# A segment softmax whose running maxima pass between steps: scan carries read from PSUM, the last carry placed by a product with one, the rescale factor spread by a row of ones

## The chip, the cores and the metric

The kernel runs on one core of a Trainium2 chip. The metric is device time in microseconds (us) of the whole launch. Three runs of the kernel before gave 1501.42, 1502.57 and 1509.48 us; the median, 1502.57 us, is the time before.

## What is computed

A graph transformer layer and a mixture of eight small feed-forward experts, both with residuals, on 3125 nodes of width 256. The part that matters here is the attention over 53125 edges, sorted by destination:

```python
qi = q[dst]; kj = k[src]; vj = v[src]          # 4 heads of 64
alpha = jnp.sum(qi * kj, axis=-1) / 8.0
m = jax.ops.segment_max(alpha, dst, num_segments=n)
ex = jnp.exp(alpha - m[dst])
denom = jax.ops.segment_sum(ex, dst, num_segments=n)
out = jax.ops.segment_sum((ex / denom[dst])[..., None] * vj, dst, num_segments=n)
```

Then come the skip product, layer norms, a GELU feed-forward, the experts with batch norm and the last residual. The diff touches none of these.

## The kernel before

`build` runs three parts in sequence: `project` (keys and values to DRAM, order of the tiles), `attend` (attention, the only one that the diff touches) and `tail` (all the rest).

**Steps and groups.** `attend` walks 232 steps. A step covers two tiles of 128 edges and one block of 128 destination nodes. Eight steps make a group (`CP = 8`), 29 groups in all. In the code `j % CP` is the place of a step in its group, and `m` is the group before the current one. All loops are unrolled; each engine has its own order of instructions, written by hand, and semaphores join them. For each step:

- GpSimd (POOL) issues two indirect DMAs (line 690) that gather key and value rows into `ring`. It waits until VectorE has multiplied the step eight earlier (`s_prod`) and TensorE has summed the one 24 earlier (`s_agg`).
- TensorE (PE) expands the queries of the block to the edges, six products into `psQ` (line 784, function `expand`); in `rest` it then sums the weighted values of the step sixteen earlier into `psA` (line 810).
- VectorE (DVE) multiplies queries and keys (`prod`, line 982), makes the one-hot matrix `oh` for the sum (line 1000), adds `psA` to the accumulator (line 1016) and reduces `prod` to `alpha` (line 1022).
- ScalarE (ACT) weights the value rows (line 764).

**The chain of maxima.** While group `m+1` is multiplied, the segment maxima of group `m` are made in pieces, one or two a step, by `maximum` on VectorE and by `rest` on TensorE. TensorE transposes the scores to 64 rows (4 heads, 16 tiles) of 128 edges in `psM`; `F1` is a scan along each row; the last element of each row goes by a product into `tails`, a row in bank `psR`; a scan of `tails` gives `carry`; the product of `inh` (a copy of `carry`) with `one` turns it into a column of `psR`. VectorE copies that column to `cin` (line 927), and the scan `F2` starts each row from it (line 930). The same goes backward: `B1`, `heads`, `back`, `iv`, a column of `psR`, the copy `bin_` (line 954), the scan `Gm` (line 957). TensorE transposes `Gm` back (line 835), `dif` is the score less its maximum, and ScalarE takes its exponential. The first element of `tails` holds the last carry of the group before; VectorE writes it with a copy (line 953) behind the wait for `T_IV`.

**The rescale.** If the first segment of a group began in the one before, the accumulator's row is scaled by `fx`. VectorE makes a one-hot row `oh0` (line 950), a product of `oh0` with `fx` puts the factor on that node's partition (line 839), and `fac` adds `noh`, which is 0 at the node and 1 elsewhere (line 966).

**Order inside a step on VectorE.** After `prod` comes piece 0 of `maximum`, then `oh`, piece 1, the accumulator's addition, piece 2, and `alpha`. Pieces are named by (step in the group, piece): `cin` is at (3, 0); `oh0`, `tails` and `bin_` are at (5, 0); `F2` and `Gm` are at (3, 1) and (5, 1). On TensorE each piece follows the sums of its step, and the next `expand` follows the piece. `s_mv` counts VectorE's pieces, `s_mp` TensorE's.

Of the kernel before, what the change touches and what calls it, by code (L numbers as in the profile page):

```python
# [24 lines left out]
ALU = mybir.AluOpType  # L25
# [3 lines left out]
P = 128  # L29
N, HID, E = 3125, 256, 53125  # L30
H, D = 4, 64
FF = 4 * HID
NB, BP = 25, 128
# [12 lines left out]
W = LT * CP  # L46
CR = 4
RING = CR * CP
R = H * W
# [41 lines left out]
def project(nc, ctx, io, keep):  # L91
# [436 lines left out]
(V_ALPHA, V_F1, V_CARRY, V_INH, V_CIN, V_F2, V_B1, V_BACK, V_IV, V_FD, V_FMIN, V_OH0, V_NEXT, V_BIN, V_G,  # L528
 V_DIFF, V_FAC) = range(1, 18)
NV = 17  # L530
# [4 lines left out]
def attend(nc, ctx, io, keep):  # L535

    c = ExitStack()
    with c:
        def sb(name, shape, dt=F32):
            return c.enter_context(nc.sbuf_tensor(name, shape, dt))  # L540
# [11 lines left out]
        dstR, valN = keep["dstR"], keep["valN"]  # L552
# [8 lines left out]
        oh0 = sb("oh0", [1, BP])  # L561
# [9 lines left out]
        cin = sb("cin", [R, 1])  # L571
        bin_ = sb("bin_", [R, 1])
# [197 lines left out]
        def _(pe):  # L770
# [18 lines left out]
            def rest(i, j, fresh):  # L789
# [29 lines left out]
                if jj == 1:  # L819
                    pe.wait_ge(s_mv, NV * m + V_F1)  # L820
                    nc.tensor.matmul(tails[:, :, 1:W + 1], F1[:, P - 1:P], ident[0:R, 0:R], start=True, stop=True).then_inc(s_mp, 1)
# [14 lines left out]
                if jj == 6:  # L836
                    pe.wait_ge(s_fx, m + 1)
                    pe.wait_ge(s_mv, NV * m + V_DIFF)
                    nc.tensor.matmul(psM[0:BP, 400:400 + H], oh0[:, :], fx[:, :], start=True, stop=True).then_inc(s_mp, 1)
# [26 lines left out]
        def _(dve):  # L866
            nc.vector.memset(psM[0:R, 2 * P:2 * P + 1], 0.0).then_inc(s_set, 1)
            nc.vector.memset(tails, NEG).then_inc(s_set, 1)
            nc.vector.memset(heads, NEG).then_inc(s_set, 1)
            dve.wait_ge(s_set, 3)  # L870
# [24 lines left out]
            def maximum(i, j, part):  # L895
# [8 lines left out]
                def seen(n):  # L904
                    dve.wait_ge(s_mv, mv + n)
# [19 lines left out]
                if at == (3, 0):  # L925
                    dve.wait_ge(s_mp, mp + T_CARRY)
                    nc.vector.tensor_copy(cin[:, :], psR[0:R, 128:129]).then_inc(s_mv, 1)
                if at == (3, 1):
                    seen(V_CIN)
                    nc.vector.tensor_tensor_scan(out=F2[:, :], data0=nrow[:, 0:P], data1=psM[0:R, 0:P], initial=cin[:, 0:1],  # L930
                                                 op0=ALU.add, op1=ALU.max).then_inc(s_mv, 1)
# [15 lines left out]
                if at == (5, 0):  # L947
                    seen(V_FD)
                    nc.vector.tensor_scalar(fm[:, :], fd[:, :], 0.0, None, ALU.min).then_inc(s_mv, 1)
                    nc.vector.tensor_scalar(oh0[:, :], iotaF[0:1, 0:BP], dstR[0:1, bass.ds(W * m, 1)], None,  # L950
                                            ALU.is_equal).then_inc(s_mv, 1)
                    dve.wait_ge(s_mp, mp + T_IV)
                    nc.vector.tensor_copy(tails[:, :, 0], carry[:, :, W]).then_inc(s_mv, 1)
                    nc.vector.tensor_copy(bin_[:, :], psR[0:R, 384:385]).then_inc(s_mv, 1)
                if at == (5, 1):
                    seen(V_BIN)
                    nc.vector.tensor_tensor_scan(out=Gm[:, ::-1], data0=psM[0:R, P + 1:2 * P + 1][:, ::-1], data1=F2[:, ::-1],
                                                 initial=bin_[:, 0:1], op0=ALU.add, op1=ALU.max).then_inc(s_mv, 1)
# [4 lines left out]
                if at == (7, 0):  # L963
                    dve.wait_ge(s_mp, mp + T_FAC)
                    at_noh = (j // CP - 1) % CR
                    nc.vector.tensor_scalar(fac[:, :], psM[0:BP, 400:400 + H], noh[:, at_noh:at_noh + 1], None,
                                            ALU.add).then_inc(s_mv, 1)
# [1024 lines left out]
```

## Time and profile before

| | |
|---|---|
| median of three runs | 1502.57 us |
| profiled execution, its own time | 1504.69 us |
| its span, first to last instruction | 1502.9 us |
| TensorE busy | 1247.5 us, 83% |
| VectorE busy | 1078.1 us, 72% |
| GpSimd busy | 930.9 us, 62% |
| ScalarE busy | 810.3 us, 54% |
| TensorE's mean granted clock | 0.933 |

The profiled execution is 2.1 us above the median, and 1.8 us of it lie outside the span. Busy shares are means over the whole run. The attention runs from about 115 to 858 us of the span, so stretches of it are read apart. Where a row says that a wait was ended by "remote", the semaphore's update was recorded but could not be matched to an instruction; "issue" means that no recorded update ended it.

### The profile page before, as it was taken

What the parts mean: (1) busy time and instruction counts of PE and PEld (TensorE: products, weight loads), DVE (VectorE), ACT (ScalarE), POOL (GpSimd) and SP (SyncE); (2) the same over time, 40 slices, a digit from 0 to 9 for tenths busy, and PEclk for the clock granted to TensorE, in tenths of its full rate; (3) what the DMA queues carried; (4) which work ended last, traced back from release to release, by engine and by line L of the source; (5) the groups of instructions that cost most, each with busy time, mean ns of one, the idle gap of its engine ahead of it and who ended that gap; (6) DMA issues with size and microseconds to landing.
All of it is one profiled execution on the core that took longest, in us unless ns stands there. A gap on an engine that the chain in (4) does not pass through costs nothing. (4 is left out here: it accounts for less than half of the span.)

```text
span 1502.9 us, 24128 instructions
## 1 busy us (share of the span) xinstructions
PE 1247.5 (83%) x6835; PEld 966.9 (64%) x6835; DVE 1078.1 (72%) x2557; ACT 810.3 (54%) x2534; POOL 930.9 (62%) x883
## 2 busy tenths in 40 slices
PE   7988776677767677667657889999999999999998
PEld 3444454454445444444445578889898899999998
DVE  7647877777777787777868779886766665656655
ACT  1356766556666766566657654565543344444443
POOL 3365566656666665666665556866765477667765
PEclk9999879888898898998988999999999999999999
DMA  7477766666666666666665120101000000000002
GB/s 222 162 218 210 224 192 192 178 180 185 199 186 199 178 199 174 201 172 197 184 180 166 31 75 29 52 27 40 9 15 22 1 22 15 8 22 15 1 12 76
DMA packets 74072, 175.40 MB, mean 117 GB/s; under 512 B 11500, under 2 KB 36651, under 8 KB 73945
## 3 DMA queue, kind: packets, MB, share of 16 engines
q0 software_dynamic: 37632, 124.28, 29.6%
q1 hardware_dynamic: 34641, 48.25, 9.6%
q10 hardware_dynamic: 1672, 1.33, 0.3%
q8 instruction: 61, 1.00, 0.3%
q14 instruction: 66, 0.54, 0.1%
HBM read 159.91 MB, written 13.91 MB: 116 GB/s over the span
## 5 line engine op out<-in xcount | busy, mean ns | idle before, releaser
L690 POOL DMA_INDIRECT ring<-kv_rows,idx x464 | 466.5, 1005 | 296.4 <-issue 116.6
L764 ACT ACTIVATE ring<-ring 128x64 f32<-128x64 f32 x1800 | 442.1, 336 | 17.2 <-issue 16.1
L1287 POOL TENSOR_TENSOR wm<-k_gf,wm 128x512 fp32r<-128x512 f32 (+1 forms) x224 | 264.0, 1181 | 147.1 <-DVE wm L1786 147.1
L1386 ACT ACTIVATE k_gf<-psF,k_scT 128x512 f32<-128x512 f32 (+1 forms) x224 | 164.0, 733 | 258.3 <-PE psF L1557 258.3
L1786 DVE CAST wm<-k_gf 128x512 fp32r<-128x512 f32 (+1 forms) x224 | 168.8, 758 | 158.7 <-ACT k_gf L1386 157.0
L810 PE MATMUL psA<-ring,oh 128*128 128x260 f32 x912 | 274.1, 429 | 7.5 <-DVE k_acc L1016 7.1
L784 PE MATMUL psQ<-k_q,ohT 128*128 x1392 | 225.3, 304 | 58.7 <-issue 58.2
L982 DVE TENSOR_TENSOR prod<-psQ,ring 128x512 f32<-128x512 f32 x232 | 157.4, 678 | 89.5 <-remote 59.9
L784 PEld LDWEIGHTS psQ<-k_q,ohT 128*128 128x128 bf16 x1392 | 131.9, 105 | 115.7 <-issue 86.0
L810 PEld LDWEIGHTS psA<-ring,oh 128*128 128x128 f32 x912 | 178.0, 217 | 36.5 <-issue 8.5
L1022 DVE TENSOR_REDUCE alpha<-prod 128x8 f32<-128x512 f32 x232 | 155.6, 671 | 0.2
L1016 DVE TENSOR_TENSOR k_acc<-k_acc,psA 128x260 f32 x232 | 93.6, 403 | 15.4 <-PE psA L810 12.3
L1279 POOL TENSOR_TENSOR gT<-k_gf,gT 128x512 fp32r<-128x512 f32 (+1 forms) x56 | 74.1, 1325 | 38.8 <-ACT gT L1375 38.7
L1801 DVE SCALAR_TENSOR_TENSOR k_acc<-psO,wt,k_acc 128x256 f32<-128x256 f32 x200 | 84.8, 473 | 9.4 <-PE psO L1575 9.3
L1000 DVE TENSOR_TENSOR oh<-k_iotaF,k_dstR 128x256 f32<-128x256 f32 x217 | 88.3, 407 | 0.0
L1374 ACT ACTIVATE k_gf<-psF,b1c 128x512 f32<-128x512 f32 (+1 forms) x56 | 36.0, 642 | 77.3 <-PE psF L1512 77.2
L1532 PE MATMUL psO<-wm,gT 128*128 128x256 f32 x200 | 58.9, 294 | 0.0
L749 ACT ACTIVATE nrow<-psM 64x128 f32<-64x128 f32 x29 | 7.8, 270 | 93.4 <-remote 43.7
L1534 PE MATMUL psO<-wm,gT 128*128 128x256 f32 x200 | 57.0, 285 | 0.0
L1533 PE MATMUL psO<-wm,gT 128*128 128x256 f32 x200 | 56.9, 285 | 0.0
L846 PE MATMUL psA<-k_wqs,k_acc 128*128 128x512 f32 x100 | 49.3, 617 | 8.0 <-ACT qst L715 4.0
L755 ACT ACTIVATE ring<-dif 128x64 f32<-128x64 f32 x29 | 9.7, 334 | 85.6 <-DVE dif L961 60.8
(284 smaller groups left out, 2671.9 us busy)
## 6 DMA issues: line engine op xcount, KB each, us to landing
ohT<-step_destinations SPq DMA_DIRECT2D x29, 512.0 KB
ring<-kv_rows,idx POOLq DMA_INDIRECT x464
kv_rows<-kvst SPq DMA_DIRECT2D x25, 260.0 KB, 2.4
we<-in_L_ffn_W SPq DMA_DIRECT2D x16, 256.0 KB, 2.8
residual<-qst SPq DMA_DIRECT2D x25, 128.0 KB
xs<-in_x SPq DMA_DIRECT2D x2, 1024.0 KB, 8.8
resin<-residual SPq DMA_DIRECT2D x4, 512.0 KB
we<-in_L_ffn_Wo SPq DMA_DIRECT2D x8, 256.0 KB, 2.7
```

Of the source, the lines that this page charges most:

```text
L690: nc.gpsimd.indirect_dma_start(out=ring[:, LT * (j % CP) + k, j // CP:j // CP + 2, :].rearrange("p t e -> p (t e)"), out_offset=None, in_= ...
L764: last = nc.scalar.activation(row[:, 0:D], row[:, 0:D], ACT.Copy, scale=row[:, D:HW_])
L784: last = nc.tensor.matmul(psQ[j % NQ][:, k * HID:(k + 1) * HID], ohT[par][:, w * P:(w + 1) * P], q3[:, part, bass.ds(blk, 1), :].rearrange ...
L810: last = nc.tensor.matmul(psA[sj % NA][0:BP, 0:HALFW], onehot(b, k), ring[:, LT * (sj % CP) + k, sj // CP, :], start=(k == 0), stop=(k == ...
L982: nc.vector.tensor_tensor(prod[:, j % 2, :].rearrange("p (k d) -> p k d", k=LT), psQ[j % NQ][:, :].rearrange("p (k d) -> p k d", k=LT), ri ...
L1000: nc.vector.tensor_tensor(oh[:, sj % NO, :, :], iotaF[:, 0:BP].unsqueeze(1).broadcast_to([P, LT, BP]), dstR[:, bass.ds(LT * bo, LT)].unsqu ...
L1016: nc.vector.tensor_tensor(row, row, psA[sj % NA][0:BP, 0:HALFW], ALU.add).then_inc(s_acc, 1)
L1022: nc.vector.tensor_reduce(alpha[:, q % 2, :, LT * jj:LT * jj + LT].rearrange("p h w -> p w h"), prod[:, j % 2, :].rearrange("p (k h d) -> ...
L1287: nc.gpsimd.tensor_tensor(low[:, i % 2, m, 0:w], gf[:, n % 4, 0:w], high[:, i % 2, m, 0:w], ALU.subtract).then_inc(s_gl, 1)
L1386: nc.scalar.activation(gf[:, n % 4, 0:cols(g)], ps, ACT.Relu, bias=bias, scale=scale).then_inc(s_ev, 1)
L1786: nc.vector.tensor_copy((h1h if layer == 1 else h2h)[:, i % 2, m, 0:w], gf[:, n % 4, 0:w]).then_inc(s_dh, 1)
L1801: last = nc.vector.scalar_tensor_tensor(out=x1(t), in0=psO[n % 3][:, (u % 2) * HID:(u % 2 + 1) * HID], scalar=wt[:, t, e:e + 1], in1=x1(t) ...
```

## The change

Four VectorE instructions of each group go: the copies `cin` and `bin_` (the scans take their `initial` straight from the column in `psR`), the one-hot row `oh0` (a constant row of ones, set once, stands in its place, and `fac` takes the larger of the factor and `noh` in place of their sum), and the copy of the last carry into `tails`. In its place TensorE writes that element by a product of `carry` with `one`, just ahead of the product that fills the rest of `tails`, in 28 of the 29 groups. The waits for `T_CARRY` and `T_IV` move from the copies to the scans, one `oh` later. `fx` is at most 1, so the larger of `fx` and 0 or 1 is what the sum with the one-hot row gave.

```diff
@@ tensor engine, function rest
                 if jj == 1:
                     pe.wait_ge(s_mv, NV * m + V_F1)
+                    if m:
+                        nc.tensor.matmul(tails[:, :, 0], one[0:1, 0:1], carry[:, :, W], start=True, stop=True)
                     nc.tensor.matmul(tails[:, :, 1:W + 1], F1[:, P - 1:P], ident[0:R, 0:R], start=True, stop=True).then_inc(s_mp, 1)
...
-                    nc.tensor.matmul(psM[0:BP, 400:400 + H], oh0[:, :], fx[:, :], start=True, stop=True).then_inc(s_mp, 1)
+                    nc.tensor.matmul(psM[0:BP, 400:400 + H], orow[:, :], fx[:, :], start=True, stop=True).then_inc(s_mp, 1)
@@ vector engine, function maximum
-                if at == (3, 0):
+                if at == (3, 1):
                     dve.wait_ge(s_mp, mp + T_CARRY)
-                    nc.vector.tensor_copy(cin[:, :], psR[0:R, 128:129]).then_inc(s_mv, 1)
-                if at == (3, 1):
-                    seen(V_CIN)
-                    nc.vector.tensor_tensor_scan(out=F2[:, :], data0=nrow[:, 0:P], data1=psM[0:R, 0:P], initial=cin[:, 0:1],
+                    nc.vector.tensor_tensor_scan(out=F2[:, :], data0=nrow[:, 0:P], data1=psM[0:R, 0:P], initial=psR[0:R, 128:129],
...
-                    nc.vector.tensor_scalar(oh0[:, :], iotaF[0:1, 0:BP], dstR[0:1, bass.ds(W * m, 1)], None,
-                                            ALU.is_equal).then_inc(s_mv, 1)
+                if at == (5, 1):
                     dve.wait_ge(s_mp, mp + T_IV)
-                    nc.vector.tensor_copy(tails[:, :, 0], carry[:, :, W]).then_inc(s_mv, 1)
-                    nc.vector.tensor_copy(bin_[:, :], psR[0:R, 384:385]).then_inc(s_mv, 1)
-                if at == (5, 1):
-                    seen(V_BIN)
                     nc.vector.tensor_tensor_scan(out=Gm[:, ::-1], data0=psM[0:R, P + 1:2 * P + 1][:, ::-1], data1=F2[:, ::-1],
-                                                 initial=bin_[:, 0:1], op0=ALU.add, op1=ALU.max).then_inc(s_mv, 1)
+                                                 initial=psR[0:R, 384:385], op0=ALU.add, op1=ALU.max).then_inc(s_mv, 1)
...
-                                            ALU.add).then_inc(s_mv, 1)
+                                            ALU.max).then_inc(s_mv, 1)
```

VectorE's order before, in the sixth step of a group (here `oh` at line 950 is `oh0`, at line 1000 the one-hot matrix; `SCALAR_TENSOR_TENSOR` is how the order names a scan):

```order
L982 TENSOR_TENSOR prod<-psQ,ring 128x512 [waits s_alpha,s_qe,s_kv5]
L949 TENSOR_SCALAR fm<-fd 1x4 [waits s_maxv]
L950 TENSOR_SCALAR oh<-k_iotaF,k_dstR 1x128
L953 COPY psR<-carry 1x4 [waits s_maxp]
L954 COPY bin_<-psR 64x1
L1000 TENSOR_TENSOR oh<-k_iotaF,k_dstR 128x256 [waits s_agg]
L957 SCALAR_TENSOR_TENSOR Gm<-psM,bin_,F 64x128 [waits s_maxv]
L1016 ISA [waits s_acc,s_agg]
```

And now, in the changed kernel's own line numbers:

```order
L974 TENSOR_TENSOR prod<-psQ,ring 128x512 [waits s_alpha,s_qe,s_kv5]
L946 TENSOR_SCALAR fm<-fd 1x4 [waits s_maxv]
L992 TENSOR_TENSOR oh<-k_iotaF,k_dstR 128x256 [waits s_agg]
L949 SCALAR_TENSOR_TENSOR Gm<-psM,psR,F 64x128 [waits s_maxp]
L1008 ISA [waits s_acc,s_agg]
```

Three instructions are gone, and the wait for TensorE's piece (`s_maxp`) stands behind the one-hot matrix.

TensorE's order now, in the second step of a group, changed kernel:

```order
L807 MATMUL psA<-ring,oh 128x260 [waits s_acc,s_oh,s_pv]
L807 MATMUL psA<-ring,oh 128x260
L819 MATMUL psR<-carry,k_one 1x4 [waits s_maxv]
L820 MATMUL psR<-k_ident,F 1x4x16
L777 TENSOR_LOAD k_brow [waits s_prod]
```

The product with `carry` is new and takes over the wait for `F1`; the register load behind it belongs to the next step's `expand`.

## Rows read from the trace of the kernel before

**Rows 1.** Two stretches: busy us (count) of PE, PEld, DVE, ACT, POOL; clock, DMA share, GB/s.
```profile
115.00:858.00 743.00, 527.88 (x2703) 353.65 (x2701) 567.25 (x1517) 484.67 (x1986) 460.57 (x468) 0.88 0.63 181
860.00:1503.00 643.00, 623.29 (x3817) 566.31 (x3815) 437.84 (x820) 285.02 (x452) 423.40 (x353) 0.98 0.09 27
```
**Rows 2.** The same view, the middle of the attention.
```profile
200.00:800.00 600.00, 417.20 (x2177) 283.75 (x2175) 455.19 (x1214) 388.25 (x1616) 376.48 (x374) 0.88 0.65 187
```
**Rows 3.** Who VectorE waited for, 200 to 800 us: total, times, longest.
```profile
DVE prod L982 <- remote: 53.8, 22, 5.2
DVE prod L982 <- PE psQ L784: 15.4, 8, 2.4
DVE psR L953 <- remote: 14.7, 5, 4.1
DVE k_acc L1016 <- PE psA L810: 10.9, 9, 1.6
DVE cin L927 <- remote: 7.2, 3, 3.4
...
DVE F L914 <- ACT nrow L749: 4.8, 3, 3.3
...
DVE cin L927 <- PE psR L824: 2.7, 5, 1.2
```
**Rows 4.** GpSimd's gathers, 200 to 800 us: busy, mean ns, idle before them.
```profile
L690 POOL DMA_INDIRECT ring<-kv_rows,idx x374 | 376.6, 1007 | 223.8 <-issue 92.7 <-DVE prod L982 47.7 <-PE psA L810 37.4
```
**Rows 5.** VectorE in order of time, about 525 us: start, duration, idle before.
```profile
525.21 0.27 DVE L950 TENSOR_SCALAR oh<-k_iotaF,k_dstR 1x128 f32<-1x128 f32 x1
525.40 0.15 DVE L953 COPY psR<-carry 1x4 f32<-1x4 f32 x1
525.47 0.14 DVE L954 COPY bin_<-psR 64x1 f32<-64x1 f32 x1
525.54 0.40 DVE L1000 TENSOR_TENSOR oh<-k_iotaF,k_dstR 128x256 f32<-128x256 f32 x1
525.87 0.47 DVE L957 TENSOR_TENSOR_SCAN Gm<-psM,bin_,F 64x128 f32<-64x128 f32 x1
```
**Rows 6.** VectorE in order of time, about 443 us.
```profile
442.58 0.69 DVE L982 TENSOR_TENSOR prod<-psQ,ring 128x512 f32<-128x512 f32 x1 [3.17 <-remote]
443.19 0.14 DVE L927 COPY cin<-psR 64x1 f32<-64x1 f32 x1
443.26 0.41 DVE L1000 TENSOR_TENSOR oh<-k_iotaF,k_dstR 128x256 f32<-128x256 f32 x1
```
**Rows 7.** TensorE in order of time, 436 to 447 us.
```profile
435.94 0.85 PE L784 MATMUL psQ<-k_q,ohT 128*128 x6 [0.48 <-issue]
...
444.76 0.27 PE L828 MATMUL psR<-k_ident,B 64*1 64x64 f32 x2 [3.31 <-DVE B L934]
445.50 1.46 PE L784 MATMUL psQ<-k_q,ohT 128*128 x6 [0.47 <-issue]
```
**Rows 8.** Single lines of VectorE: ns min/median/max, first and last start us.
```profile
L950 DVE TENSOR_SCALAR oh<-k_iotaF,k_dstR x29: 267/268/353, 140.9 to 842.7; 1x128 f32<-1x128 f32 x29
L927 DVE COPY cin<-psR x29: 134/140/152, 131.3 to 839.8; 64x1 f32<-64x1 f32 x29
L930 DVE TENSOR_TENSOR_SCAN F<-nrow,cin,psM x29: 461/465/473, 131.4 to 840.2; 64x128 f32<-64x128 f32 x29
L914 DVE TENSOR_TENSOR_SCAN F<-nrow,psM x29: 401/402/413, 125.4 to 837.2; 64x128 f32<-64x128 f32 x29
```
**Rows 9.** VectorE by line and form, 200 to 800 us: busy, mean ns, idle before.
```profile
L953 DVE COPY psR<-carry 1x4 f32<-1x4 f32 x23 | 3.5, 150 | 17.0 <-remote 14.7 <-PE psR L831 1.3 <-issue 1.1
L927 DVE COPY cin<-psR 64x1 f32<-64x1 f32 x23 | 3.3, 143 | 12.4 <-remote 7.2 <-PE psR L824 2.7 <-issue 2.5
```
**Rows 10.** TensorE by line, 200 to 800 us: busy, mean ns, idle before.
```profile
L824 PE MATMUL psR<-k_one,inh 1*64 1x1 f32 x48 | 7.0, 213 | 6.8 <-DVE inh L924 6.3 <-issue 0.5
L821 PE MATMUL psR<-k_ident,F 64*1 64x64 f32 x48 | 7.0, 229 | 31.5 <-DVE F L914 28.4 <-issue 3.0
```

More of the change, by code:

```diff
@@ L525, in _ @@
                     backward(t - AT_ENDS - 1)
-(V_ALPHA, V_F1, V_CARRY, V_INH, V_CIN, V_F2, V_B1, V_BACK, V_IV, V_FD, V_FMIN, V_OH0, V_NEXT, V_BIN, V_G,
- V_DIFF, V_FAC) = range(1, 18)
-NV = 17
+(V_ALPHA, V_F1, V_CARRY, V_INH, V_F2, V_B1, V_BACK, V_IV, V_FD, V_FMIN, V_G, V_DIFF, V_FAC) = range(1, 14)
+NV = 13
 (T_IN, T_TAIL, T_CARRY, T_HEAD, T_IV, T_OUT, T_FAC) = range(1, 8)
@@ L560, in attend @@
         oh = sb("oh", [P, NO, LT, BP])
-        oh0 = sb("oh0", [1, BP])
+        orow = sb("orow", [1, BP])
         prod = sb("prod", [P, 2, LT * HID])
@@ L570, in attend @@
         Gm = sb("Gm", [R, P])
-        cin = sb("cin", [R, 1])
-        bin_ = sb("bin_", [R, 1])
         carry = sb("carry", [1, H, W + 1])
@@ L869, in _ @@
             nc.vector.memset(heads, NEG).then_inc(s_set, 1)
+            nc.vector.memset(orow[:, :], 1.0)
             dve.wait_ge(s_set, 3)
```

## The prediction

> **What bounds the kernel now.** The page's first part has no engine that fills the run, so I read its stretches next. After 860 us TensorE is busy 623 of 643 us; in the attention before it, 743 us, VectorE is the busiest with 567 us, and nobody is full [rows 1]. The change lies in the attention alone, so the 643 us behind it stay as they are, and the question is what sets the pace of the 743 us ahead of them.
>
> A group of eight steps takes 25.3 us: `cin` stands in the trace 29 times, first at 131.3 us and last at 839.8 us, and 708.5 / 28 = 25.3 [rows 8]. Between 200 and 800 us VectorE is busy 455.2 of 600 us [rows 2], so 19.2 us of each group, and idle 6.1 us. Its idle time comes in few, long pieces: 30 waits of up to 5.2 us ahead of `prod`, 9 of up to 1.6 us ahead of the accumulator's addition, some in the chain of maxima [rows 3]. One of them can be followed. VectorE starts `prod` at 442.58 us after 3.17 us of nothing [rows 6]; the queries it needs stand on TensorE from 435.94 us on, for 0.85 us [rows 7]. TensorE itself then sits 3.31 us, until VectorE has made `B1` for it [rows 7]. So TensorE's result became visible late, by a cause that these rows do not name, and then each engine stood and waited for the other. Outside such pieces VectorE works without a gap.
>
> GpSimd's gathers are not what is late. Of its 223.8 us of idle time, 92.7 us are the spacing of its own issue, and most of the rest it waits for `prod` or for the sums to free a place in the ring [rows 4]. It follows the others. I read the attention as paced by VectorE's work plus the late pieces.
>
> **The change, part by part.** *Removed from VectorE.* In the sixth step `oh0` starts at 525.21 and the one-hot matrix at 525.54: the three small instructions take 0.33 us of VectorE's queue [rows 5]. In the fourth step `cin` starts at 443.19 and the next one at 443.26: 0.07 us [rows 6]. That makes 0.40 us a group, and 29 x 0.40 = 11.6 us. Their own durations are longer, 0.27 + 0.15 + 0.14 us [rows 5] and 0.14 [rows 6], because neighbours overlap; 29 x 0.70 = 20.3 us is the upper bound, if nothing overlapped. The lower bound is 0: all of it disappears into the idle time. VectorE is free of idle for 455.2 / 600 = 0.76 of the stretch [rows 2]. I take that share as what passes to the end: 0.76 x 11.6 = 8.8 us.
>
> *The two waits move behind `oh`.* VectorE was idle 17.0 us ahead of `tails` and 12.4 us ahead of `cin` in 23 groups [rows 9]. The one-hot matrix holds the queue 0.33 us, from 525.54 to 525.87 [rows 5], and can now be made during such a wait. Thirteen waits at the two places have a row: 5 and 3 that were long, and 5 of up to 1.2 us [rows 3]; together 24.6 of the 29.4 us. Hidden are 13 x 0.33 = 4.3 us, times 29 / 23 groups 5.4 us. If the other 4.8 us of waiting were hidden whole as well, it would be 9.1 x 29 / 23 = 11.5 us, the upper bound; the lower is 0. I take 0.76 of the 5.4 us, as above: 4.1 us. No engine waits longer for the moved things: `F2` and `Gm` came behind `oh` before too, and `oh` itself comes sooner for TensorE's sum.
>
> *The scans with a start value in PSUM.* No row shows one. `F1`, with a constant, takes 402 ns; `F2`, with a start value in SBUF, 465 ns [rows 8]. If a PSUM value were as cheap as a constant, two scans a group would give 29 x 2 x 0.063 = 3.7 us more. If it cost a whole read of the same column, as `cin` does in 140 ns [rows 8], they would take back 29 x 2 x 0.14 = 8.1 us. I take 0, since the nearest row is the same scan with another start value, and it already reads its data from PSUM. The Trainium skill, page "VectorE: DVE Perf Modes", section "The TRN2 errata — SBUF-src ops pay a fixed extra latency per instruction", speaks against the change here: it gives a VectorE instruction 58 cycles fixed from SBUF and 120 from PSUM at 0.96 GHz. If a start value in PSUM were charged like that, an estimate from the page is 62 / 0.96 = 65 ns a scan, 3.7 us in all to take back, and the median would come out at 1494 us. No run here shows it yet.
>
> *The new product on TensorE.* Its kin are the one-element products: 213 ns a pass [rows 10], and the two passes of the product at 444.76 take 0.27 us together [rows 7]. 28 x 0.27 = 7.6 us is the upper bound. It stands at a place where TensorE waits for VectorE, 31.5 us ahead of the products with `F1` in this stretch [rows 10], and behind it the next `expand` starts only after 0.47 us that the sequencer spends on its register [rows 7]. `carry` has been ready since the group before. It delays `tails` by up to 0.27 us, and the scan of `tails` comes a whole step later on VectorE. I take 1.0 us for all groups; the bounds are 0 and 7.6. If the cover goes, because TensorE is the late one in that step, it costs the 0.27 us.
>
> *At no cost:* `max` for `add` in `fac` is the same instruction, and the product with ones reads 128 values as `oh0` did. The one `memset` is outside the loop. ScalarE and GpSimd have the same order as before.
>
> The sum: 8.8 + 4.1 + 0 - 1.0 = 11.9 us. From the profiled execution's own 1504.69 us that gives 1492.8. It lies 2.1 us above the median of the runs, so the median should be 1490.7, which I call 1491 us. About 0.5%, 7.5 us, is what a measurement of this kernel tells from no change: faster means under 1495, slower over 1510.
>
> **The rivals.**
>
> *A, the sum holds (0.46): 1487 to 1495, likeliest 1491.* For it: VectorE is gapless between the late pieces.
>
> *B, nothing that can be measured (0.32): 1496 to 1504.* The late pieces, 6.1 us of each group, might end by something that does not depend on VectorE's work. Then a VectorE that is done 0.4 us sooner waits 0.4 us longer. ScalarE's `nrow` holds up `F1` in 3 waits, 4.8 us [rows 3], and the DMA queues are busy 0.65 of the stretch [rows 2]: such causes would swallow the gain. Only the matrices made under a wait would be left, 0 to 4 us, and the PSUM start value could eat that too. Time 1500. Against it: 39 waits have their row ahead of `prod` and the addition, for 24 groups of eight steps [rows 3], so most steps have none, and in those VectorE's work counts in full.
>
> *C, slower (0.10): 1511 to 1530.* A wait takes the place of the removed work. A faster VectorE frees the ring sooner, the gathers follow closer on each other, and DMA's share, 0.65, rises. If the late results of TensorE go with busy DMA queues, there will be more of them. One costs about 3.2 us, as ahead of `prod` at 442.58 [rows 6]. Four more in 29 groups eat up the 11.9 us; from six more on the kernel is slower by over 0.5%, and ten more, one in three groups, give 1491 + 32 = 1523. For it: the late result at 442.58 has no other cause in these rows. Against it: VectorE's speed changes by under 2%, and gathers would come that much closer only.
>
> *D, faster than the sum (0.12): 1478 to 1486.* The engines stand and wait for each other, and TensorE's clock pays for it: 0.88 in the attention against 0.98 behind it [rows 1]. At half speed the six products take 1.46 us and not 0.85 [rows 7], 0.6 us more. A share of 0.24 at half speed makes 0.88. If shorter waits took it to 0.20, that is 0.04 x 232 = 9 steps less at half speed; with the sums, which are longer than the queries, some 1.5 us each, 14 us of TensorE, of which I would see half: 1491 - 7 = 1484. The Trainium skill's page "TensorE: Matmul & The Clock Gate", section "HAM oscillation — how this bites in real kernels", has the rule that a TensorE that idles falls to half its clock. By that rule the rows agree: the six products at 445.50 come behind an idle 3.31 us and take 1.46 us.
>
> **How the numbers follow.** Likeliest is A, so 1491. The range takes in A and B, most of D and none of C: 1482 to 1505, with some 0.15 to 0.2 outside. Faster: A's 0.46 (of which a little is above 1495) and D's 0.12, 0.57. Slower: C's 0.10. Within 0.5%: 0.33.
>
> **What would show it.** In the changed kernel's profile: VectorE's busy time down by some 10 us in the attention; the spacing of `fm` to `oh` in the sixth step 0.07 us; the scans `F2` and `Gm` at 465 ns, or over 500 if PSUM is dear. The group's period should be 24.9 us. If it is 25.3 with VectorE's idle time up by the same 0.4, it was B. If VectorE's long waits are more in number, it was C. The clock at 0.90 or more would be D. I am wrong in the sum if the start value in PSUM costs more than 0.2 us a scan, or if the long waits go by the clock on the wall and not by steps.

## The result, and the profile after

The changed kernel took 1531.13 us (median of 4 runs, 1526.77 to 1535.13), the kernel before 1501.99 us beside it (4 runs, 1498.76 to 1509.48): a ratio of 1.0199, interval 1.0167 to 1.0231. It is 29 us slower, where 1491 us was predicted. The profiled execution has a time of 1534.81 us and a span of 1533.0 us, 30.1 us more than before.

The chips differ, and this has to be said ahead of everything else. On some the kernel before takes 1501 to 1503 us, as above (the same in two later series on one chip); on three others it takes 1359 to 1361 us. I call the first **late chips** and the others **prompt chips**, for a reason that the traces show further down. A ratio is always to the kernel before on the same chip and in the same series; it can differ by up to 0.3% from the quotient of the two medians.

The same stretches of the changed kernel as in [rows 1, 2]: busy us (count) of PE, PEld, DVE, ACT, POOL; then clock, DMA share, GB/s. The last stretch is TensorE's 643 us behind the attention.

```profile
115.00:858.00 743.00, 526.97 (x2636) 359.07 (x2637) 531.19 (x1333) 459.22 (x1892) 443.67 (x436) 0.82 0.63 181
200.00:800.00 600.00, 418.39 (x2134) 290.31 (x2131) 426.55 (x1074) 366.98 (x1539) 362.65 (x358) 0.82 0.62 180
890.00:1533.00 643.00, 621.30 (x3817) 564.60 (x3816) 440.40 (x820) 285.50 (x453) 426.95 (x353) 0.99 0.09 27
```

What follows the attention is as it was: TensorE is busy 621 of the last 643 us, before 623 of 643 [rows 1]. The loss is in the attention, and there less got done in the same time: GpSimd issued 358 gathers in 600 us and not 374 [rows 4].

The two scans that now start from PSUM, by line (nanoseconds least/median/most, first and last start in us):

```profile
L927 DVE TENSOR_TENSOR_SCAN F<-nrow,psR,psM x29: 465/467/477, 132.5 to 870.7; 64x128 f32<-64x128 f32 x29
L949 DVE TENSOR_TENSOR_SCAN Gm<-psM,psR,F x29: 468/469/479, 142.2 to 873.9; 64x128 f32<-64x128 f32 x29
```

They take 467 and 469 ns; with a start value in SBUF it was 465 [rows 8]. The first and last start give the group's period: (870.7 - 132.5) / 28 = 26.4 us, where it was 25.3 and 24.9 was forecast.

What GpSimd waited for stands in one row of each kernel, the gathers' over the whole run (busy, mean ns | idle ahead of them, and what ended it). First the kernel before:

```profile
L690 POOL DMA_INDIRECT ring<-kv_rows,idx x464 | 466.5, 1005 | 296.4 <-issue 116.6 <-DVE prod L982 59.4 <-ACT idx L727 50.6
```

And the changed kernel:

```profile
L687 POOL DMA_INDIRECT ring<-kv_rows,idx x464 | 471.4, 1016 | 319.9 <-issue 120.2 <-ACT idx L724 104.5 <-DVE prod L974 40.2
```

GpSimd is busy 4.9 us longer and idle 23.5 us longer ahead of its gathers, together 28.4 of the 30.1 us. This sum shows no cause: GpSimd issues from one end of the attention to the other, and whatever holds it up, its busy and idle time add up to that length. The releasers say more. Its waits for VectorE's `prod` became shorter, 59.4 to 40.2 us, and those for TensorE's sums too, 39.8 to 11.0 us; the unmatched ones ("remote") grew from 15.7 to 29.8 us. What grew by far the most is the wait for `idx`, from 50.6 to 104.5 us. `idx` is the table of row numbers of a group of eight steps that ScalarE makes (line 724), one group ahead. The number of such waits stands in the same view by that line, "who waited for it". Before:

```profile
L727 ACT ACTIVATE idx<-k_srcI x29: 199/203/217, 69.9 to 795.4; 128x16 int32<-128x16 int32 x29
...
  POOL ring L690: 50.6, 16
```

And in the changed kernel:

```profile
L724 ACT ACTIVATE idx<-k_srcI x29: 198/202/216, 70.0 to 825.8; 128x16 int32<-128x16 int32 x29
...
  POOL ring L687: 104.5, 26
```

GpSimd ran out of indices in 16 of 29 groups before, and in 26 of 29 now.

Who waited for whom in the changed kernel, 200 to 800 us (total, times, longest):

```profile
ACT nrow L746 <- remote: 118.4, 22, 6.3
DVE prod L974 <- remote: 101.8, 31, 5.3
...
POOL ring L687 <- ACT idx L724: 82.2, 21, 4.1
...
DVE F L914 <- ACT nrow L746: 19.8, 10, 3.1
DVE Gm L949 <- remote: 19.8, 8, 4.2
```

In [rows 3] `prod` had 22 such waits, 53.8 us. The same view of the kernel before has two more rows, which neither the rows ahead of the prediction nor its argument took up:

```profile
ACT nrow L749 <- remote: 43.7, 9, 6.3
...
POOL ring L690 <- ACT idx L727: 32.6, 12, 4.1
```

`nrow` on ScalarE now waits 118.4 us for TensorE's transposes under this name, and 2.5 us in a wait that names them; before it was 43.7 us so, 31.4 us in waits that name them and 11.3 us under "issue". One of these waits shows the whole thing. ScalarE (start, duration, what it did, in brackets the idle time ahead and what ended it):

```profile
443.13 0.24 ACT L728 ACTIVATE stc<-k_startN 128x64 f32<-128x64 f32 x1
449.59 0.27 ACT L746 ACTIVATE nrow<-psM 64x128 f32<-64x128 f32 x1 [6.22 <-remote]
449.77 2.00 ACT L761 ACTIVATE ring<-ring 128x64 f32<-128x64 f32 x8
451.68 0.20 ACT L724 ACTIVATE idx<-k_srcI 128x16 int32<-128x16 int32 x1
```

TensorE, the transposes that it waits for, and the products with the queries that the late `prod` multiplies:

```profile
444.68 0.27 PE L813 MATMUL psM<-k_ident,alm 128*64 128x128 f32 x1
444.79 0.27 PE L814 MATMUL psM<-k_ident,stc 128*64 128x128 f32 x1
...
457.00 0.83 PE L781 MATMUL psQ<-k_q,ohT 128*128 x6
```

GpSimd in the same time:

```profile
447.29 0.94 POOL L687 DMA_INDIRECT ring<-kv_rows,idx  x1 [0.30 <-issue]
452.15 1.23 POOL L687 DMA_INDIRECT ring<-kv_rows,idx  x1 [3.92 <-ACT idx L724]
...
461.19 0.95 POOL L687 DMA_INDIRECT ring<-kv_rows,idx  x1 [0.30 <-issue]
464.49 1.16 POOL L687 DMA_INDIRECT ring<-kv_rows,idx  x1 [2.36 <-DVE prod L974]
```

And VectorE:

```profile
449.96 0.41 DVE L914 TENSOR_TENSOR_SCAN F<-nrow,psM 64x128 f32<-64x128 f32 x1 [2.87 <-ACT nrow L746]
...
453.70 0.67 DVE L974 TENSOR_TENSOR prod<-psQ,ring 128x512 f32<-128x512 f32 x1
...
456.34 0.67 DVE L974 TENSOR_TENSOR prod<-psQ,ring 128x512 f32<-128x512 f32 x1
...
457.99 0.66 DVE L1014 TENSOR_REDUCE alpha<-prod 128x8 f32<-128x512 f32 x1
463.75 0.69 DVE L974 TENSOR_TENSOR prod<-psQ,ring 128x512 f32<-128x512 f32 x1 [5.09 <-remote]
464.36 0.15 DVE L946 TENSOR_SCALAR fm<-fd 1x4 f32<-1x4 f32 x1
464.42 0.41 DVE L992 TENSOR_TENSOR oh<-k_iotaF,k_dstR 128x256 f32<-128x256 f32 x1
```

TensorE finished the transposes at 445.06 us, and ScalarE went on at 449.59, 4.5 us later. What lies just ahead of that moment is GpSimd's last gather of a run, which ended at 448.23. It is the same 14 us later: TensorE ended this step's query products at 457.83, the last gather ends at 462.14, and `prod` starts at 463.75, 5.9 us after its products. Both signals stayed out while gathers followed each other without a pause, and arrived 1.4 and 1.6 us after the last one.

Counted over the trace, it is a pattern with exceptions. Between 200 and 800 us the changed kernel has 58 waits of VectorE and ScalarE that are longer than 2 us and ended by "remote". In all 58 the semaphore is one that TensorE counts up. 47 of them ended 1 to 2 us after the end of GpSimd's latest gather, though such moments make up only 46 of the 600 us; in the kernel before it is 23 of 31. The other eleven do not fit, and other signals of TensorE get through while gathers run: `prod` at 453.70 and 456.34 did not wait. So a part of TensorE's signals goes by GpSimd's pauses, and which part the rows do not say.

Now ScalarE's order matters. `idx` of the next group stands behind `nrow` and behind the eight weightings of a step. GpSimd needs `idx` to go on, `idx` stands behind the late signal, and the signal comes when GpSimd stops. So GpSimd must stop at the end of its indices. Here this stop costs 3.92 us, and the stop for a free place in the ring costs 2.36 us.

### The profile page after: what moved, and what is told of

Its sections match the earlier page's. It is cut to its first block and busy times, and to the rows that moved or that the text cites. A ratio compares the mean times of both kernels' runs of the same rounds, so it can differ in the third digit from the quotient of the medians.

```text
span 1533.0 us, 24125 instructions
## 1 busy us (share of the span) xinstructions
PE 1268.8 (83%) x6891; PEld 987.3 (64%) x6891; DVE 1068.6 (70%) x2442; ACT 807.2 (53%) x2534; POOL 939.8 (61%) x883
## 5 line engine op out<-in xcount | busy, mean ns | idle before, releaser
L687 POOL DMA_INDIRECT ring<-kv_rows,idx x464 | 471.4, 1016 | 319.9 <-issue 120.2
L807 PE MATMUL psA<-ring,oh 128*128 128x260 f32 x912 | 285.9, 444 | 3.6 <-DVE k_acc L1008 3.5
L781 PE MATMUL psQ<-k_q,ohT 128*128 x1392 | 237.6, 317 | 38.2 <-issue 35.6
L807 PEld LDWEIGHTS psA<-ring,oh 128*128 128x128 f32 x912 | 186.8, 228 | 32.6 <-ACT ring L761 3.7
L781 PEld LDWEIGHTS psQ<-k_q,ohT 128*128 128x128 bf16 x1392 | 138.7, 108 | 94.0 <-issue 61.1
L834 PE MATMUL psM<-k_ident,Gm 64*128 64x64 f32 x29 | 9.6, 332 | 92.7 <-DVE Gm L949 92.7
L834 PEld LDWEIGHTS psM<-k_ident,Gm 64*128 64x128 f32 x29 | 4.7, 163 | 105.1 <-DVE Gm L949 104.1
L819 PE MATMUL psR<-carry,k_one 1*1 1x4 f32 x56 | 5.3, 163 | 66.7 <-DVE F L914 66.7
L1524 PE MATMUL psO<-wm,gT 128*128 128x256 f32 x200 | 59.1, 295 | 0.7 <-POOL gT L1271 0.7
```

The source lines that it names most:

```text
L687: nc.gpsimd.indirect_dma_start(out=ring[:, LT * (j % CP) + k, j // CP:j // CP + 2, :].rearrange("p t e -> p (t e)"), out_offset=None, in_= ...
L781: last = nc.tensor.matmul(psQ[j % NQ][:, k * HID:(k + 1) * HID], ohT[par][:, w * P:(w + 1) * P], q3[:, part, bass.ds(blk, 1), :].rearrange ...
L807: last = nc.tensor.matmul(psA[sj % NA][0:BP, 0:HALFW], onehot(b, k), ring[:, LT * (sj % CP) + k, sj // CP, :], start=(k == 0), stop=(k == ...
```

## The experiments

### The parts alone, and the indices first (a prompt chip, kernel before 1360.9 us)

*PSUM starts*: the kernel before, with the scans' start values in PSUM only. *Ones row*: with the row of ones and the larger of factor and `noh` only. *Carry product*: with the product for the last carry only.

The core of *PSUM starts* and, below the line of dots, of *carry product*, both on VectorE:

```diff
-                    nc.vector.tensor_copy(bin_[:, :], psR[0:R, 384:385]).then_inc(s_mv, 1)
-                                                 initial=bin_[:, 0:1], op0=ALU.add, op1=ALU.max).then_inc(s_mv, 1)
+                                                 initial=psR[0:R, 384:385], op0=ALU.add, op1=ALU.max).then_inc(s_mv, 1)
...
-                    nc.vector.tensor_copy(tails[:, :, 0], carry[:, :, W]).then_inc(s_mv, 1)
```

> The kernel before with one part of the change: the two scans start from PSUM and the copies cin and bin_ are gone; the wait for the forward column moves behind the one-hot matrix, the wait for the backward one stays ahead of it, with the copy into tails. Theory L (late indices: the 29 us lost are GpSimd's longer waits for the gather indices, which ScalarE makes behind nrow, and any part that takes time out of VectorE can tip the groups into that pattern): a time anywhere between 1500 and 1530 us, and whatever it is, the excess over 1502 us equals the growth of GpSimd's idle time ahead of the gathers (296 us before, 320 in the changed kernel). Theory P (the new product on TensorE costs it): no product here, so 1502 us or less. Theory S (a start value in PSUM slows the chain): 1515 us or more.

> The kernel before with another part alone: the one-hot row oh0 is gone, a constant row of ones and a maximum stand in its place. VectorE loses 0.19 us a group. Theory L: 1500 to 1530 us, with the excess over 1502 equal to the growth of GpSimd's idle time. Theory P and theory S: 1502 us or a little less, since neither the product nor the start values are here.

> The kernel before with the third part alone: the copy of the last carry into tails is gone, TensorE writes it by a product ahead of the one with F1. VectorE loses 0.07 us a group, TensorE gains two passes. Theory P: 1520 us or more, most of the loss. Theory L: near 1502 us unless the pattern tips, since VectorE's order hardly changes. Theory S: 1502 us.

*Indices first*: the changed kernel, in which ScalarE makes `idx` one step sooner, ahead of its wait for the transposes.

```diff
-                if j % CP == 1 and live(i, j - 1, fresh, -CP):
+                if j % CP == 0 and live(i, j, fresh, -CP):
```

> The changed kernel, with one thing moved on ScalarE: the indices of the next group are made one step earlier, ahead of nrow, which waits for TensorE's transposes. Theory L: GpSimd's waits for the indices (82 us between 200 and 800 us) go to nearly 0 and the time falls from 1531 to 1505 us or below. Theory P, theory S, and a theory in which TensorE's late results alone cost the time: GpSimd only waits elsewhere, and the time stays within 5 us of 1531.

Measured: 1364.78 us, 1.0036 (1.0019 to 1.0054); 1362.42, 1.0008 (0.9992 to 1.0025); 1355.63, 0.9967 (0.9949 to 0.9986); and the indices first 1361.0, 1.0003 (0.9986 to 1.0021). All of them are near 1360 us, as the kernel before is on this chip, so the loss to be explained wasn't there. Nothing follows for the 29 us; for a prompt chip the parts are worth +0.4, +0.1 (not told from nothing) and -0.3%.

### The changed kernel as it is, and three variants (another prompt chip, kernel before 1359.5 us)

*Changed again* has no edit. *Before, indices first* is the kernel before with the diff just shown. *Padded* is the changed kernel with four VectorE instructions whose results nobody reads, of the sizes and at the places of those removed; they read and write SBUF, also where the removed ones had a side in PSUM. *Short lead* is the changed kernel with GpSimd held to five steps ahead of `prod`.

The additions of *padded* in the sixth step (the fourth stands in the fourth step), and below the dots *short lead*, where `LEAD` is 5:

```diff
+                    nc.vector.tensor_scalar(pada[:, :], iotaF[0:1, 0:BP], dstR[0:1, bass.ds(W * m, 1)], None, ALU.is_equal)
+                    nc.vector.tensor_copy(padb[:, :], carry[:, :, W])
+                    nc.vector.tensor_copy(padc[:, :], F1[:, 0:1])
...
-                if not (fresh and j < CP):
-                    pool.wait_ge(s_prod, step - CP + 1)
+                if not (fresh and j < LEAD):
+                    pool.wait_ge(s_prod, step - LEAD + 1)
```

> The changed kernel as it is, again, beside the kernel before on one chip. In the last runs the kernel before took 1361 us and not 1502, with GpSimd issuing gathers almost without a pause. Theory G (where signals are not late GpSimd's issue is the bound, 16 gathers a group at 1.25 us, and VectorE's work is hidden): on a chip where the kernel before takes 1361 us, the changed one is within 0.5% of it, 1354 to 1368 us. Theory L (late indices tip in only where signals are late): on a chip where the kernel before takes about 1500 us, the changed one is at 1525 to 1535. Theory P (the product on TensorE costs by itself): slower by 1 to 2% on either.

> The kernel before, with the next group's indices made one step earlier on ScalarE, ahead of nrow. Theory L: on a chip where the kernel before takes about 1500 us GpSimd loses its waits for indices (50 us in the first profile) and the time falls by 10 us or more. Theory G: on a chip at 1361 us no change, within 4 us. A theory in which the late signals alone set the time: no change on either.

> The changed kernel with four idle VectorE instructions, of the forms and at the places of the four that the change removed; they feed nothing and wait for nothing. Theory L with a phase set by VectorE's pace: where the kernel before takes about 1500 us, this one comes back to 1500 to 1510. Theory P, S or moved waits: it stays at 1525 or more. At 1361 us for the kernel before: all say within 0.5%.

> The changed kernel, with GpSimd held to 5 steps ahead of prod in place of 8. Theory R (signals of TensorE and ScalarE go out late while GpSimd issues gathers without a pause, and come about 1.5 us after its last one): where the kernel before takes about 1500 us, the late pieces become shorter and more, and GpSimd's pauses come from prod and not from the indices, so the time changes by over 10 us, either way. A theory in which the late signals have nothing to do with GpSimd's run: pieces as long as before, time within 10 us of the changed kernel. On a chip at 1361 us: GpSimd waits for prod now and then, 1361 to 1400 us.

Measured: changed again 1361.86 us, 1.0015 (1.0003 to 1.0027); before, indices first 1359.51, 0.9998 (0.9985 to 1.0011); padded 1368.66, 1.0061 (1.0040 to 1.0082); short lead 1366.70, 1.0054 (1.0035 to 1.0073). The same program that lost 2% loses 0.15% here. In its trace the gathers' row reads:

```profile
L687 POOL DMA_INDIRECT ring<-kv_rows,idx x464 | 466.1, 1005 | 164.2 <-issue 116.5 <-PE psA L807 18.9 <-DMA kv_rows<-kvst 14.2
```

A piece of its timeline of GpSimd:

```profile
450.23 0.95 POOL L687 DMA_INDIRECT ring<-kv_rows,idx  x1 [0.30 <-PE psA L807]
451.49 0.94 POOL L687 DMA_INDIRECT ring<-kv_rows,idx  x1 [0.30 <-issue]
452.73 0.95 POOL L687 DMA_INDIRECT ring<-kv_rows,idx  x1 [0.30 <-issue]
```

The gathers follow each other 1.25 us apart. Sixteen of them make 20.0 us, and the scan `Gm` comes every (700.1 - 127.6) / 28 = 20.4 us:

```profile
L949 DVE TENSOR_TENSOR_SCAN Gm<-psM,psR,F x29: 469/469/480, 127.6 to 700.1; 64x128 f32<-64x128 f32 x29
```

So here GpSimd's issue is the pace, and VectorE waits for gathers to land (200 to 600 us):

```profile
DVE prod L974 <- DMA ring<-kv_rows,idx: 34.4, 24, 3.9
```

The idle time ahead of the gathers is 164 us and not 320. And the late signals are gone. In the twelve profiles from prompt chips, 200 to 600 us, no wait of VectorE or ScalarE over 2 us is ended by "remote", and every update that TensorE makes is recorded within 0.02 us of the end of its instruction (441 of 441 in this one). In the changed kernel's first profile, 200 to 800 us, 444 updates are recorded for 515 such instructions, and 202 of them come over 1 us after the latest one that had ended. That is what the names of the two kinds of chip mean: on a prompt chip TensorE's signals arrive while GpSimd issues, on a late chip many do not.

### A late chip, its own variations, and more copies (kernel before 1501.45 us)

*Before again* has no edit. *One-hot in four* is the kernel with the carry product in which VectorE makes the large one-hot matrix `ohT` in four pieces of 512 columns, because long gathers in the traces lay beside it. *More copies* adds to the kernel before, and to the changed one, 25 copies of 1 MB from DRAM to DRAM, one a group.

```diff
+                        sp.dma_start(io["extra"][cc, :, :], io["x"][0:1024, :]).then_inc(s_extra, 16)
```

> The kernel before as it is, for its profile on a chip such as the last two. Theory G (GpSimd's issue is the bound there: the time is the sum of the gathers' own durations plus their spacing, and about 675 us behind the last one): the sum of the 464 gathers lies near 467 us, GpSimd's idle time ahead of them near 162 us, and VectorE's waits ahead of prod are for the gathers. Theory L's late pieces, if the chip is one where this kernel takes about 1500 us: idle time near 296 us.

> The kernel before with the carry by a product (the part that measured 0.9967 alone), and the expansion matrix ohT made in four instructions of 512 columns, spread over a step, in place of one of 2048. Theory G with the gathers stretched by that one instruction (they take 946 ns, but up to 1.6 us where they overlap it): the sum of the gathers' durations falls by 5 to 15 us and the time with it, to 1345 to 1352 us where the kernel before takes 1360. If the stretch has nothing to do with it: within 3 us of 1356, or slower, since VectorE has three more instructions a group.

> The kernel before with 25 copies of 1 MB from DRAM to DRAM beside it, one a group, that nothing reads. Theory D (TensorE's signals go out late when the DMA queues are full, as the rival C of the prediction has it): late pieces of 2 us and more appear in every group, idle time of GpSimd goes from 162 to 250 us and more, and the time to 1450 or more. If late signals are a property of the chip and not of the queues: the gathers land later, VectorE waits for them ahead of prod, but TensorE's signals come on time; 1365 to 1450 us.

> The changed kernel with the same 25 copies. If full queues bring the late signals back and theory L holds, it is slower than e10 by 1 to 2%, as on the first chip (1531 against 1502). If not, it is within 0.5% of e10.

Measured: before again 1500.95 us, 0.9991; one-hot in four 1511.83, 1.0077 (1.0059 to 1.0095); before with copies 1507.72, 1.0025 (0.9992 to 1.0059); changed with copies 1526.58, 1.0197 (1.0134 to 1.0261). The stretch from 200 to 800 us, before again and before with copies:

```profile
200.00:800.00 600.00, 416.28 (x2182) 280.79 (x2181) 457.87 (x1220) 391.52 (x1630) 378.06 (x377) 0.89 0.66 188
```

```profile
200.00:800.00 600.00, 417.38 (x2153) 283.24 (x2152) 453.58 (x1207) 385.15 (x1605) 373.37 (x371) 0.87 0.73 227
```

The copies raise the DMA share from 0.66 to 0.73 and 188 to 227 GB/s, and the time by nothing that can be told from no change (the interval reaches to 0.6%). The late waits over 2 us are 23 without and 21 with the copies, and the prompt chips, with a share of 0.79, have none. So the late signals don't go by the load of the DMA queues, as rival C supposed. The changed kernel was not run here without the copies. With them it is 2% slower than the kernel before without them, and 1.3% slower (1526.58 and 1507.72) than the kernel before with the same copies, which is the fair pair; GpSimd's waits for `idx` are 73.3 against 55.8 us in the two. So the change loses on this late chip too, by somewhat less than on the first. The matrix in four pieces shortened the gathers, to 458.4 us from 465.4, and yet the time rose: the length of a gather is not what is lost on a late chip. This kernel has the carry product in it, and waits for `idx` 44.7 us, as good as the 42.5 us of *before again*.

### Four kernels once more (a third prompt chip, kernel before 1360.6 us)

Indices first, short lead, padded and PSUM starts, the same programs as above.

> The changed kernel with the next group's indices made one step earlier on ScalarE, once more. Where the kernel before takes about 1500 us: theory L (the 2% are GpSimd's waits for indices) says that these waits, 82 us between 200 and 800 us, go to under 10 and the ratio to before falls from 1.020 to 1.003 or less. Theory T (the late signals set the pace; GpSimd's place of waiting is only where it shows) says that GpSimd waits for prod or the sums instead and the ratio stays at 1.015 or more. Where before takes 1360 us: 1.000, as measured.

> The changed kernel with GpSimd held to 5 steps ahead of prod in place of 8, once more. Where the kernel before takes about 1500 us: theory R (the signals come about 1.5 us after GpSimd stops, so a shorter run ends them sooner) says late pieces of at most 3 us, more of them, and a time that differs from the changed kernel's by over 10 us, more likely down. If lateness does not depend on GpSimd's run: pieces of 5 us stay and the ratio is 1.02 or more. Where before takes 1360 us: 1.005, as measured.

> The changed kernel with four idle VectorE instructions in place of the four removed, once more. Where the kernel before takes about 1500 us: if the loss comes by VectorE's pace (theory V), the ratio falls to 1.005 or less; if it comes by the start values in PSUM, the moved waits or the product, it stays at 1.015 or more. Where before takes 1360 us: 1.006, as measured.

> The kernel before with the scans started from PSUM alone, once more. Where the kernel before takes about 1500 us: if the start values or the forward wait behind the one-hot matrix cost the time, 1.010 to 1.020; theory V, with a third of the removed time here, 1.003 to 1.010; if only the product or the backward wait costs it, 1.000. Where before takes 1360 us: 1.0036, as measured.

They were meant for a late chip and came upon a prompt one. Measured: 1362.84 us, 1.0010 (0.9995 to 1.0024); 1364.09, 1.0030 (1.0016 to 1.0045); 1365.92, 1.0052 (1.0032 to 1.0073); 1364.65, 1.0034 (1.0018 to 1.0050). The first readings hold, and decide nothing on the 29 us.

### The indices first on a late chip (kernel before 1503.3 us)

The edits are those of *indices first* and *one-hot in four*.

> The changed kernel with the next group's indices made one step earlier on ScalarE, a third time. Where the kernel before takes about 1500 us: theory L says GpSimd's waits for indices go to under 10 us and the ratio to 1.003 or less; theory T says it waits elsewhere and the ratio stays at 1.015 or more. Where before takes 1360 us: 1.000 to 1.001, as measured twice.

> The kernel before with the carry by a product and the expansion matrix made in four instructions, a second time. Where the kernel before takes 1360 us, theory G: the gathers' durations sum to about 460 us, 5 us less than with the product alone, and the time falls by as much, to 1348 to 1352 us, ratio 0.991 to 0.995. If VectorE or the landing of the gathers is the bound there: 0.997 or more. Where before takes 1500 us: 1.008, as measured.

Measured: indices first 1492.62 us (8 runs, 1489.07 to 1496.45), 0.9933 (0.9904 to 0.9962); one-hot in four 1510.27, 1.0047 (1.0024 to 1.0069). One line of ScalarE's program, moved up by one step, takes the changed kernel from 1531 us (on the first chip, 1.0199) to 1493 us (0.9933), and it is the fastest of all on a late chip. Its gathers' row, its table `idx` and its waits from 200 to 800 us:

```profile
L687 POOL DMA_INDIRECT ring<-kv_rows,idx x464 | 462.4, 997 | 288.4 <-issue 119.2 <-DVE prod L974 95.9 <-PE psA L807 46.7
```

```profile
L724 ACT ACTIVATE idx<-k_srcI x29: 197/199/215, 69.9 to 779.8; 128x16 int32<-128x16 int32 x29
...
  POOL ring L687: 3.3, 1
```

```profile
ACT nrow L746 <- remote: 49.6, 10, 6.3
...
DVE prod L974 <- remote: 32.7, 15, 4.9
```

GpSimd waits once for `idx`, 3.3 us, and not 26 times, 104.5 us. Signals still come late (`nrow` waits up to 6.3 us), but GpSimd now stops for a place in the ring: its waits for `prod` and for the sums are 95.9 and 46.7 us, where they were 40.2 and 11.0. The 101.2 us of waits for `idx` that went came back in part, and 31.5 us less idle time and 9.0 us less in the gathers are left. Together they are the 40 us by which the span is shorter (1493.1 and 1533.0), as they must be. The scan `F2`:

```profile
L927 DVE TENSOR_TENSOR_SCAN F<-nrow,psR,psM x29: 466/470/477, 134.8 to 830.7; 64x128 f32<-64x128 f32 x29
```

gives a period of (830.7 - 134.8) / 28 = 24.9 us. That is the forecast figure, reached by another way than the forecast's.

## Why the prediction was wrong

**The step that failed** is "GpSimd's gathers are not what is late", with "It follows the others", and from it the factor 0.76 for what passes to the end. On a late chip it's the other way round in most of the long pieces: a signal of TensorE that VectorE or ScalarE needs comes when GpSimd stops. GpSimd's waits for `idx` rose from 50.6 to 104.5 us, and with `idx` made one step sooner they fell to 3.3 us and the time to 1493 us. I had also read [rows 4] too lightly: of the 131.1 us there that aren't issue, `prod` and the sums make 85.1. The rows show only the three largest releasers; the other 46.0 us are 32.6 for `idx` and 13.4 "remote" (over the whole run `idx` has 50.6 us in 16 groups), and they are absent from my argument. And I had stopped at "a cause that these rows do not name" for the late pieces [rows 6, 7], though they make 75.7 us of VectorE's 144.8 us of idle time in that stretch [rows 2, 3].

**At no cost: "ScalarE and GpSimd have the same order as before"** is true of the order, and wrong as a reason. Their order held a loop (GpSimd, `idx`, `nrow`, TensorE's signal, GpSimd): GpSimd waited for `idx` in 16 groups before and in 26 now.

**Rival C**, slower by more late waits, had the kind of result right and two things wrong. The unmatched waits did rise, `prod`'s from 22 to 31 and `nrow`'s from 9 to 22 (with the matched ones `nrow` waited 86 us before and 121 now); at the two places whose wait was moved they stayed as they were (5 and 3 before, 8 and 1 now). But its mechanism was busier DMA queues, and the copies speak against that: the share even fell, 0.65 to 0.62, in the changed kernel. And it named `prod` and the ring, not `nrow` and `idx`. That its 1523 us lies near the measured 1531 is therefore luck as to the cause.

**Removed from VectorE, 8.8 us, and the waits behind `oh`, 4.1.** VectorE's busy time fell by 9.5 us over the run (1078.1 to 1068.6), and `fm` to `oh` in the sixth step is 464.36 to 464.42, as forecast. That neither reached the end is the failure above. With the indices first the changed kernel is 10.7 us faster than the kernel before, where the sum said 11.9. I can't count this near agreement as proof of the sum: what the indices first are worth to the kernel before on a late chip wasn't tried, and it had 50.6 us of the same waits.

**The start value in PSUM, 0 us**, was right: 2 to 4 ns a scan, 0.2 us in all. From the Trainium skill's page "VectorE: DVE Perf Modes", section "The TRN2 errata — SBUF-src ops pay a fixed extra latency per instruction", which gives 58 and 120 fixed cycles, I had estimated 65 ns. The measurement decides: this difference isn't added for a start value in scans that already read their data from PSUM.

**The product on TensorE, 1.0 us.** One pass takes 162 ns, less than the 213 of its kin. But the cover was misread: the product stands behind the wait for `F1` and not in it, so the 31.5 us of waiting hide none of it. TensorE waits for `F1` in nearly every one of the 28 groups (53 waits, counted for the weight load and the product apart), and `tails` comes later by the product. What that is worth at the end, no run on a late chip shows; on a prompt chip the kernel with the product alone is 0.3% faster.

```profile
L819 PE MATMUL psR<-carry,k_one x56: 162/163/163, 155.8 to 868.6; 1*1 1x4 f32 x56
its engine sat idle before it (us, times) until:
  DVE F L914: 144.5, 53
```

**Rival D**: the granted clock went the other way, 0.88 to 0.82 in the attention. With the indices first it is back at 0.88, though nothing on TensorE was edited, so it follows from the stops.

**Rival B** is what a prompt chip shows in its result, no change that matters: the pace there is GpSimd's issue, and less work on VectorE is more of waiting.

**What stays open.** Why 0.4 us less on VectorE, or any other part of the change, closes the loop in ten more groups. An account that fits is phase: where the late stops fall in a group decides whether `idx` is made in time. It is not shown. Putting idle instructions in the place of the removed ones would test it, but these two runs fell on prompt chips. So did *short lead*, which would show whether a shorter run of gathers shortens the lateness, and the parts alone, so that which part tips it on a late chip isn't known; the carry product came to a late chip only together with the one-hot in four, twice, at 1.0077 and 1.0047 and without more waits for `idx` to speak of (44.7 and 46.2 us). That the whole 29 us go through `idx` isn't shown either: taking away 101.2 us of such waits gave 39.9 us, and at that rate the 53.9 us that the change added would be 21 us, an estimate. And no run here shows why a chip is late, or by which path GpSimd's gathers hold up TensorE's signals.

## What to carry to other kernels

Ask of each engine's waits which other engine's wait they stand behind, also where the diff doesn't touch it: a table that a gather needs must not be made behind a wait for the result of that gather's own consumers. Read the idle time of the engine that you call a follower by its releaser over the whole run; a small row in a loop (50.6 us here) is a price that a change elsewhere can double. And time a change on more than one chip: this one is +2.0% on one and +0.15% on another, and one moved line makes -0.7% of the +2.0%.

## What the runs showed of the hardware

On late chips a semaphore update of TensorE can stay out for several us while GpSimd issues indirect gathers back to back: in the changed kernel the 50 unmatched waits over 2 us of `prod` and `nrow` ended 1.6 to 6.4 us after the end of the TensorE instruction that they needed. Of all 58 such waits 47 ended 1 to 2 us after the latest gather. On prompt chips the same programs have none; the kernel takes 1360 us and not 1501 to 1531, at least 9% less, with the DMA queues busy 0.79 of the time (*changed again*, 200 to 600 us) and not 0.66 (*before again*).

A gather of 128 rows takes 0.95 us to issue, with 0.30 us between two, on both kinds of chip; single ones take up to 2.2 us. On prompt chips small changes of the time go with the sum of these durations. Padded and changed kernel on one chip:

```profile
L691 POOL DMA_INDIRECT ring<-kv_rows,idx x464 | 473.3, 1020 | 163.1 <-issue 111.2 <-PE psA L811 20.7 <-DMA kv_rows<-kvst 14.1
```

against 466.1 us above. That is 7.2 us more in the gathers, with the idle time nearly the same, and 6.8 us more in the median. The same padded kernel on the third prompt chip had 468.7 us, so that a part of this changes from run to run. Over the twelve profiles from prompt chips the sum goes from 462.6 to 473.3 us and the profiled time from 1357.2 to 1368.6 us; the least and the most of both belong to the same two kernels, the carry product alone and padded. What makes a single gather long, no run here shows.
